# One-core attention and mixture-of-experts kernel: the first expert tile's products placed between the last two attention pairs' products

## The chip, the cores and the metric

The kernel runs on one core of a Trainium2 chip. The core has five engines that follow their own instruction streams and meet through semaphores: TensorE (PE, with its weight loads shown apart as PEld), VectorE (DVE), ScalarE (ACT), GpSimd (POOL) and SyncE (SP). The metric is the time of one execution in microseconds on the device.

## The reference

The input x holds 128 sequences of 64 rows of width 128. Everything is in float32.

```python
x = x + attention(layernorm(x), ctx, ctx, Wq, Wk, Wv, Wo, bo, mask)   # 16 heads of 64, causal
z = layernorm(x + attention...) * ln_g + ln_b        # ffn's own layernorm of the sum
probs = softmax(z @ rW + rb)                         # 8 experts
w = top-2 of probs, normalised
hid = gelu(z @ W1[e] + b1[e]);  outs = hid @ W2[e] + b2[e]
x = x + sum over the two chosen experts of w * outs
```

## The kernel before

**Attention.** The 8192 rows are worked off as 64 *pairs* of sequences (128 rows each), four pairs to a *group*, 16 groups. The program numbers pairs from 0, and `NP` is 64, so the last two pairs are NP-2 = 62 and NP-1 = 63. For each pair TensorE makes the value products (`V` units), the scores (L1045), the transposes of the probabilities of the pair before (`T` units, L997), the products of those with the values (`attend`, L1014, 64 small 64x64 products) and the output projection (`project`, L1029, 8 products of float32 that the profile lists as 16 rows). VectorE subtracts the row maxima from the scores (L1325, L1327) and counts on the semaphore `shifted`; ScalarE takes the exponential (L773); VectorE normalises (L1333 to L1337), counting on `probs`. ScalarE copies the transposes to `pT` (L754) and the result of `attend` to `oT` (L768). VectorE adds the projection to the residual (`add_attention`, L1318). Routing of the rows to experts (`route_a`, `route_b`, `route_c`) and the scatter of normed rows to `slots` (POOL L618, one indirect DMA for each 128 rows) run in the same groups.

**Experts.** The sorted rows lie in `slots` in tiles of 256 rows, 67 tiles, each of one expert. For tile s: SP loads it to `zin` (L456); TensorE transposes it (`rows_t`, L1148, 2 products) and signals `ct_ps`; ScalarE copies the high part to `z_hi` (`hi_part`, L839); VectorE makes the low part `z_lo` (`lo_part`, L1634, signals `cl_lo`) and copies the expert's weights (`weights`, L1625 to L1627, signals `wc_ok`); TensorE makes the first products (`up`, three-part split, L914, L915 and L918 with `Ah` and `Al`, 6 products, signals `up_ps`); ScalarE takes gelu (`hidden`, L846, signals `gl_ok`); TensorE makes the second products (`down`, L1166 and L1171, signals `dn_ps`); ScalarE copies them out (`results`, L854, signals `yv_ok`); POOL scatters them to `mixed` (L702, two indirect DMAs). VectorE also works out where the rows go (`destinations` and `places`, L1640 to L1651).

**Order.** Each engine's order is the order in which the code is written. At the end of attention TensorE does, for the last group's fourth pair: the routing's rank products, `fold_b1` (L1081, 16 products one column wide), V, `attend` of pair 62, then tile 0's `rows_t`, `project` of pair 62, the T units of pair 63, `attend` of pair 63, tile 0's `up`, `project` of pair 63, and then the tiles. VectorE does `weights` and `lo_part` of tile 0 after the normalisation of pair 63. PSUM has 8 banks: banks 0 to 4 are a ring for the units of attention, banks 5 and 6 (`s_ps`) hold scores, bank 7 the projection. The buffers of the tiles (`zin`, `w_f`, `hid`, `z_hi`) lie over buffers of attention that are no longer read.

## Time and profile before

| | |
|---|---|
| three runs | 1013.84, 1015.98 and 1017.59 us |
| median | 1015.98 us |
| the profiled execution's own time | 1021.77 us |
| its span from first to last instruction | 1020.0 us |
| mean granted TensorE clock | 0.959 |
| busy PE / DVE / ACT / POOL | 909.9 / 730.4 / 617.6 / 463.9 us |

The profiled execution has 1.77 us around its span, and is 5.79 us above the median of the three runs. A busy share is an average over stages. TensorE has 660.45 us busy in the first 700 us, 94%, and less in the expert tiles behind it.

### The profile page before, as it was taken

The numbers are of one execution on the slowest core, as the hardware profiler recorded it, in microseconds if no ns is written. First come the engines' busy times: TensorE is split into PE (matmuls) and PEld (weight loads), VectorE is DVE, ScalarE is ACT, GpSimd is POOL, SyncE is SP. The second block draws the span as 40 slices with busy tenths as digits, with TensorE's granted clock in tenths as the row PEclk, the third lists the DMA queues.
The fourth block names the chain that finished last, engine by engine and source line by source line (L and its number), as shares of the span: only waits on it lengthen the run. The fifth ranks groups of instructions, "written<-read, shape, count | busy, mean of one in ns | idle before, by whom it ended". The sixth has DMA issues, their size and how long they took to land.

```text
span 1020.0 us, 36053 instructions
## 1 busy us (share of the span) xinstructions
PE 909.9 (89%) x13532; PEld 794.6 (78%) x13532; DVE 730.4 (72%) x2240; ACT 617.6 (61%) x1330; POOL 463.9 (45%) x571
## 2 busy tenths in 40 slices
PE   8999999999999999999999999999887889887870
PEld 6788888888888888888888888888776778776760
DVE  5887876778777777778778778786756565445773
ACT  5785667567656766667666756766444444354662
POOL 3432644435364543436364443533445545544562
PEclk9999999999999999999999999999987889998985
DMA  8000010101010010101001010001022322224555
GB/s 257 14 23 21 26 36 8 36 5 36 8 39 28 13 34 8 36 5 36 23 24 31 10 37 6 26 8 36 17 64 74 92 82 77 68 71 136 170 186 193
DMA packets 53401, 53.59 MB, mean 53 GB/s; under 512 B 6983, under 2 KB 46705, under 8 KB 53329
## 3 DMA queue, kind: packets, MB, share of 16 engines
q1 hardware_dynamic: 44891, 35.84, 12.4%
q0 software_dynamic: 8128, 16.79, 4.9%
q8 instruction: 36, 0.59, 0.2%
q14 instruction: 36, 0.29, 0.1%
q10 hardware_dynamic: 310, 0.08, 0.0%
HBM read 30.52 MB, written 22.17 MB: 52 GB/s over the span
## 4 chain that ended last, share of the span: by engine, by line
PE 75%; issue 7%; DVE 6%; ACT 4%; another core or an unknown queue 4%; DMA 2%; DVEq 1%; POOL 0%; SPq 0%; POOLq 0%; ACTq 0%
PE bank L1029 12%; PE bank L914 10%; PE bank L918 10%; PE bank L915 9%; PE bank L1045 9%; PE bank L1014 7%; PE bank L997 5%; PE bank L1171 4%; PE bank L1201 2%; PE bank L967 1%; PE bank L1148 1%; PE bank L942 1%; ACT pr L846 1%; DMA c_in<-in_ctx_dram 1%
## 5 line engine op out<-in xcount | busy, mean ns | idle before, releaser
L914 PE MATMUL bank<-in_h,Ah 128*128 128x256 f32 x646 | 208.0, 322 | 19.6 <-DVE Al L1634 17.1
L773 ACT ACTIVATE pr<-pr 128x512 f32<-128x512 f32 x128 | 80.4, 628 | 231.0 <-DVE pr L1327 231.0
L702 POOL DMA_INDIRECT mixed<-kf,ix_i x134 | 133.1, 994 | 125.1 <-DVE ix_i L1651 90.8
L726 ACT ACTIVATE kf<-bank 128x512 f32<-128x512 f32 x256 | 156.6, 612 | 8.1 <-PE bank L918 4.1
L914 PEld LDWEIGHTS bank<-in_h,Ah 128*128 128x128 f32 x646 | 125.7, 195 | 27.3 <-DVE Al L1634 21.4
L618 POOL DMA_INDIRECT slots<-zrow,slot_ix x120 | 126.1, 1051 | 45.3 <-issue 27.9
L1325 DVE TENSOR_REDUCE mx<-bank 128x8 f32<-128x512 f32 x128 | 87.7, 685 | 81.1 <-PE bank L1045 81.0
L918 PE MATMUL bank<-in_h,Al 128*128 128x256 f32 x512 | 145.0, 283 | 0.0
L915 PE MATMUL bank<-in_l,Ah 128*128 128x256 f32 x512 | 144.6, 282 | 0.0
L1045 PEld LDWEIGHTS bank<-kf 64*64 64x64 f32 x4096 | 81.8, 134 | 66.8 <-issue 65.6
L1029 PE MATMUL bank<-wo_s,oT 128*128 128x128 f32 x1024 | 132.7, 283 | 0.6 <-ACT oT L768 0.6
L1045 PE MATMUL bank<-kf 64*64 64x64 f32 x4096 | 102.9, 224 | 31.1 <-issue 30.4
L553 POOL TENSOR_TENSOR idle_p<-half 128x1 f32<-128x1 f32 x120 | 28.9, 243 | 214.5 <-DVE slot_ix L1423 174.9
L1029 PEld LDWEIGHTS bank<-wo_s,oT 128*128 128x128 f32 x1024 | 120.6, 193 | 5.2 <-ACT oT L768 1.0
L1337 DVE TENSOR_TENSOR pr<-pr,ri 128x512 f32<-128x512 f32 x128 | 114.1, 892 | 4.4
L1171 PE MATMUL bank<-kf,pr 128*128 128x128 f32 x536 | 85.2, 307 | 18.4 <-ACT pr L846 18.4
L558 POOL TENSOR_TENSOR rs<-ve,half 128x4 f32<-128x4 f32 (+1 forms) x32 | 43.6, 1361 | 125.0 <-DVE ve L1259 89.5
L915 PEld LDWEIGHTS bank<-in_l,Ah 128*128 128x128 f32 x512 | 97.9, 191 | 0.0
L918 PEld LDWEIGHTS bank<-in_h,Al 128*128 128x128 f32 x512 | 97.2, 190 | 0.0
L1171 PEld LDWEIGHTS bank<-kf,pr 128*128 128x128 f32 x536 | 71.6, 208 | 27.4 <-ACT pr L846 19.8
L1014 PEld LDWEIGHTS bank<-pT,vf 64*64 64x64 f32 x4096 | 69.9, 136 | 28.5 <-issue 26.0
L1327 DVE TENSOR_TENSOR pr<-bank,mx 128x512 f32<-128x512 f32 x128 | 88.5, 692 | 4.4
(202 smaller groups left out, 2009.6 us busy)
## 6 DMA issues: line engine op xcount, KB each, us to landing
kf<-slots SPq DMA_DIRECT2D x67, 130.0 KB
kf<-mixed SPq DMA_DIRECT2D x11, 512.0 KB
xs<-in_x_dram SPq DMA_DIRECT2D x16, 256.0 KB
c_in<-in_ctx_dram SPq DMA_DIRECT2D x16, 256.0 KB
out_dram<-xs SPq DMA_DIRECT2D x16, 256.0 KB
mixed<-kf,ix_i POOLq DMA_INDIRECT x134
vf<-mixed SPq DMA_DIRECT2D x4, 512.0 KB
slots<-zrow,slot_ix POOLq DMA_INDIRECT x120
```

The source lines that it names most:

```text
L618: pool.indirect_dma_start(out=slots, out_offset=bass.IndirectOffsetOnAxis(ap=ix[:, k, t:t + 1], axis=0), in_=rows[:, t, :], in_offset=None ...
L702: pool.indirect_dma_start(out=mixed, out_offset=bass.IndirectOffsetOnAxis(ap=ix_i[buf][:, j:j + 1], axis=0), in_=y_sb[buf][:, j, :], in_of ...
L726: act.activation(kfs[par][:, 2 * u:2 * u + 2, :], ring[gr.bank(name)].rearrange("p (h t) -> p h t", h=2), ACT.Copy).then_inc(act_ev, 1)
L914: pe.matmul(ps, lh, rh, start=True, stop=False)
L915: pe.matmul(ps, lh, rl, start=False, stop=False)
L918: return pe.matmul(ps, ll, rh, start=False, stop=True)
L1014: last = pe.matmul(into[b][place, S * j:S * j + S], vf[par][seq, 2 * j + h2, :], pT[seq, j, 64 * (h2 ^ b):64 * (h2 ^ b) + 64], start=True, ...
L1029: last = pe.matmul(o_ps[:, 0:D], oT[:, j, :], wo_s[:, j, :], start=(j == 0), stop=(j == H // 2 - 1))
L1045: last = pe.matmul(s_ps[b][place, S * j:S * j + S], kfs[par][dims, j, toks], kfs[par][dims, H // 2 + j, toks], start=False, stop=True, ski ...
L1171: last = pe.matmul(into[:, j, :], hid[deep][:, c, j * P:(j + 1) * P], w_f[deep][:, c * D:(c + 1) * D], start=False, stop=(c == FC - 1), sk ...
L1327: dve.tensor_tensor(by_seq(par, t), src, mx[:, par, hs].unsqueeze(2).to_broadcast([P, 8, S]), ALU.subtract).then_inc(shifted, 1)
L1337: dve.tensor_tensor(by_seq(par, t), by_seq(par, t), ri[:, par, hs].unsqueeze(2).to_broadcast([P, 8, S]), ALU.mult).then_inc(probs, 1)
```

## The change

The change reorders the end of attention and makes these helpers available earlier in the code. TensorE: `rows_t` of tile 0 moves to before `fold_b1`, and the wait for the last pair's `shifted` with it; `up` of tile 0 stands before `project` of pair 62; `rows_t` of tile 1 and `down` of tile 0 stand before `attend` of pair 63, and `up` of tile 1 right behind it. ScalarE and VectorE follow: tile 0's `hi_part` stands inside the last group, gelu of tile 0 before the copies of pair 63's T units, and the tile 0 weights and low part before the last normalisation. Tile 1's transposes and first products share bank 3; tile 0's second products go to bank 5.

```diff
+        def turned_at(s, deep):
+            return ({0: s_ps[0], 1: bank[3]}.get(s, bank[deep % 2]) if isinstance(s, int) else bank[deep % 2])[:, 0:TILE]
+        def results_at(s, deep):
+            into = s_ps[0] if isinstance(s, int) and s == 0 else bank[4 + deep % 2]
@@ ScalarE
                     exp_half(n, par, 1)
+                    if i == 3 and last:
+                        hi_part(0, 0)
...
-            hi_part(0, 0)
+            hidden(0, 0)
             for t in range(2):
                 t_unit(tail, f"T0{t}", NP - 1, t)
+            hi_part(1, 1)
+            results(0, 0)
             for b in range(2):
                 heads_unit(tail, f"O0{b}")
-            hidden(0, 0)
-            for s in range(1, NT):
+            for s in range(2, NT):
@@ TensorE
                     if i == 3 and last:
+                        pe.wait_ge(shifted, 2 * NP)
+                        rows_t(0, 0, s_ps[0])
                         fold_b1(gr)
...
-            pe.wait_ge(shifted, 2 * NP)
-            rows_t(0, 0, s_ps[0])
+            up(0, 0, s_ps[1])
             project(NP - 2, group_of(NG - 1, last=True).done("O31", 0))
             for t in range(2):
                 t_half(tail, f"T0{t}", NP - 1, 1, t)
+            rows_t(1, 1, bank[3])
+            down(0, 0)
             heads_free(tail, 0)
             attend(tail, 0, 1)
-            up(0, 0, s_ps[1])
+            up(1, 1, bank[3])
             project(NP - 1, tail.done("O01", 0))
-            rows_t(1, 1, bank[1])
-            down(0, 0)
-            for s in range(2, NT):
+            rows_t(2, 2, bank[0])
+            for s in range(3, NT):
                 tile_products(s)
@@ VectorE
                     if i == 3 and last:
+                        e = expert_of(0)
+                        first_weights(e)
+                        lo_part(0, 0)
                         dve.wait_ge(unit, gr.done("RB"))
...
+                        dve.wait_ge(dve_ev, gr.done("RB", 1))
+                        weights(0, 0, e)
                     normalize_half(n, par, 0)
...
-            weights(0, 0, expert_of(0))
-            lo_part(0, 0)
+            destinations(0, 0)
+            places(0, 0)
             add_attention(NP - 2)
             weights(1, 1, expert_of(1))
-            destinations(0, 0)
-            places(0, 0)
+            lo_part(1, 1)
             add_attention(NP - 1)
             for s in range(ADD_FROM):
                 tile_in(s, s)
```

The next listing is TensorE's order before, from pair 63's scores to tile 1's first products (`in_h,Ah` and `Al,Ah` are the first products of a tile, `kf,pr` the second, `ident,kf` a tile's transposes; `x8` of `wo_s,oT` is one `project`).

```order
L1081 MATMUL bank<-vec_cols,w_raw 128x1 x16
L914 MATMUL bank<-Vh,in_h 128x512
L915 MATMUL bank<-Vl,in_h 128x512
L918 MATMUL bank<-Vh,in_l 128x512
L1014 MATMUL bank<-pT,vf 64x64 x32
L1148 MATMUL bank<-ident,kf 128x128 x2
L1029 MATMUL bank<-wo_s,oT 128x128 x8
L997 MATMUL bank<-ident,pr 128x128 x8
L1014 MATMUL bank<-pT,vf 64x64 x32
L914 MATMUL bank<-in_h,Ah 128x256
```

The same stretch of TensorE in the changed kernel.

```order
L1096 MATMUL bank<-ident,kf 128x128 x2
L1087 MATMUL bank<-vec_cols,w_raw 128x1 x16
L920 MATMUL bank<-Vh,in_h 128x512
L921 MATMUL bank<-Vl,in_h 128x512
L924 MATMUL bank<-Vh,in_l 128x512
L1020 MATMUL bank<-pT,vf 64x64 x32
L920 MATMUL bank<-in_h,Ah 128x256
```

Behind those first products of tile 0 (six rows in all, of which the first stands above) the changed kernel goes on so.

```order
L1035 MATMUL bank<-wo_s,oT 128x128 x8
L1003 MATMUL bank<-ident,pr 128x128 x8
L1096 MATMUL bank<-ident,kf 128x128 x2
L1176 MATMUL bank<-w_b,ones_b 128x256
L1181 MATMUL bank<-kf,pr 128x128 x4
L1020 MATMUL bank<-pT,vf 64x64 x32
L920 MATMUL bank<-in_h,Ah 128x256
```

No product is added or removed: two sets of transposes, two sets of first products and one of second products change places. On VectorE, between the last group's `slot_ix` and the normalisation (`sm`, `ri`, `pr`), the changed kernel has this.

```order
L1432 CAST slot_ix<-rq 128x8
L1526 TENSOR_LOAD tile_e_i
L1526 ISA x2
L1550 ISA
L1550 COPY Ah<-w_parts 128x512
L1542 TENSOR_TENSOR Al<-bank,in_h 128x256
L1595 TENSOR_TENSOR experts<-bank,vec_cols 128x8x2
L1534 ISA
L1534 COPY kf<-experts 128x258
L1535 ISA
L1535 COPY w_b<-b_parts 3x128
L1342 TENSOR_REDUCE sm<-pr 128x8
```

Before, only the addition to `experts` stood between `slot_ix` and that normalisation; the others came behind it.

## Rows read from the trace of the kernel before

**Rows 1.** The page: the chain that ended last, share of the span by engine

```profile
PE 75%; issue 7%; DVE 6%; ACT 4%; another core or an unknown queue 4%; DMA 2%; DVEq 1%; POOL 0%; SPq 0%; POOLq 0%; ACTq 0%
```

**Rows 2.** Two stretches: length, busy (x instructions) of PE, PEld, DVE, ACT, POOL; PEclk, DMA

```profile
734.00:746.00 12.00, 6.96 (x97) 5.88 (x94) 3.21 (x12) 3.35 (x8) 6.73 (x7) 0.78 0.16 51
746.00:752.00 6.00, 6.00 (x42) 5.63 (x40) 2.18 (x11) 3.60 (x8) 0.00 (x0) 0.79 0.03 5
```

**Rows 3.** TensorE in order of time: start us, us, line, [idle before <-releaser]

```profile
727.35 3.71 PE L1081 MATMUL bank<-vec_cols,w_raw 128*128 128x1 f32 x32
...
732.07 1.99 PE L1014 MATMUL bank<-pT,vf 64*64 64x64 f32 x64
733.99 0.69 PE L1148 MATMUL bank<-ident,kf 128*128 128x128 f32 x2
735.25 2.05 PE L1029 MATMUL bank<-wo_s,oT 128*128 128x128 f32 x16 [0.57 <-ACT oT L768]
...
739.27 1.01 PE L1014 MATMUL bank<-pT,vf 64*64 64x64 f32 x34 [1.09 <-ACT pT L754]
741.48 0.28 PE L1014 MATMUL bank<-pT,vf 64*64 64x64 f32 x2 [1.20 <-issue]
742.92 0.45 PE L1014 MATMUL bank<-pT,vf 64*64 64x64 f32 x3 [1.17 <-issue]
744.33 0.97 PE L1014 MATMUL bank<-pT,vf 64*64 64x64 f32 x25 [0.96 <-issue]
745.23 0.58 PE L914 MATMUL bank<-in_h,Ah 128*128 128x256 f32 x1
...
746.68 2.80 PE L1029 MATMUL bank<-wo_s,oT 128*128 128x128 f32 x16
...
749.63 0.28 PE L1166 MATMUL bank<-w_b,ones_b 3*128 3x256 bf16 x1
...
750.83 0.38 PE L1148 MATMUL bank<-ident,kf 128*128 128x128 f32 x2
...
752.52 0.39 PE L914 MATMUL bank<-in_h,Ah 128*128 128x256 f32 x1 [0.37 <-DVE Al L1634]
```

**Rows 4.** The chain in order of time, an earlier pair's attend

```profile
720.48 1.09 PE bank L1014 x64
```

**Rows 5.** VectorE in order of time

```profile
727.45 0.69 DVE L1327 TENSOR_TENSOR pr<-bank,mx 128x512 f32<-128x512 f32 x1
...
733.69 0.69 DVE L1337 TENSOR_TENSOR pr<-pr,ri 128x512 f32<-128x512 f32 x1
...
749.51 0.29 DVE L1318 TENSOR_TENSOR xs<-bank,xs 128x128 f32<-128x128 f32 x1 [10.03 <-PE bank L1029]
...
750.25 0.42 DVE L1634 TENSOR_TENSOR Al<-bank,in_h 128x256 fp32r<-128x256 f32 x1
...
752.06 0.40 DVE L1634 TENSOR_TENSOR Al<-bank,in_h 128x256 fp32r<-128x256 f32 x1
```

**Rows 6.** ScalarE in order of time, around tile 0's gelu

```profile
745.32 1.09 ACT L768 ACTIVATE oT<-bank 128x512 f32<-128x512 f32 x2 [6.10 <-PE bank L1014]
746.42 1.28 ACT L846 ACT_TABLE_LOAD   x1
747.72 0.84 ACT L846 ACTIVATE pr<-bank,kf 128x256 f32<-128x256 f32 x2
```

**Rows 7.** POOL in order of time, its last scatter to slots and first to mixed

```profile
741.91 0.96 POOL L618 DMA_INDIRECT slots<-zrow,slot_ix  x1 [0.30 <-issue]
752.19 0.96 POOL L702 DMA_INDIRECT mixed<-kf,ix_i  x1 [9.31 <-DVE ix_i L1651]
```

**Rows 8.** SP's loads of tiles 0 to 3

```profile
705.20 3.65 SPq L456 DMA_DIRECT2D kf<-slots  x4
```

**Rows 9.** Who waited for whom, PE, 0 to 700 us: total us, times, longest

```profile
PE bank L1045 <- issue: 29.3, 73, 0.5
```

**Rows 10.** Who waited for whom, all engines, 724 to 1020 us

```profile
ACT pr L846 <- remote: 27.9, 8, 5.1
```

More of the change, by code:

```diff
@@ L779, in seed, with hi_part @@
                                scale=NEG).then_inc(seeded, 1)
+            def hi_part(s, deep):
+                act.wait_ge(ct_ps, s + 1)
+                if not isinstance(s, int) or s >= DEEP:
+                    act.wait_ge(up_ps, s - DEEP + 1)
+                act.activation(z_hi[deep], turned_at(s, deep), ACT.Copy).then_inc(ch_hi, 1)
             def group(g, first=False, last=False):
@@ L1083, in fold_b1, with rows_t @@
                 last.then_inc(unit, 1)
+            def rows_t(s, deep, into):
+                pe.wait_ge(zi[deep], 4 * (s - deep) + 16)
+                if not isinstance(s, int) or s >= 2:
+                    pe.wait_ge(cl_lo, s - 1)
+                for j in range(TJ):
+                    last = pe.transpose(into[:, j * P:(j + 1) * P], zin[deep][:, j, 0:D], ident[:, :])
+                last.then_inc(ct_ps, 1)
             def group(g, first=False, last=False):
@@ L1142, in _ @@
             group(NG - 1, last=True)
-            def rows_t(s, deep, into):
-                pe.wait_ge(zi[deep], 4 * (s - deep) + 16)
-                if not isinstance(s, int) or s >= 2:
-                    pe.wait_ge(cl_lo, s - 1)
-                for j in range(TJ):
-                    last = pe.transpose(into[:, j * P:(j + 1) * P], zin[deep][:, j, 0:D], ident[:, :])
-                last.then_inc(ct_ps, 1)
             def up(s, deep, into):
@@ L1162, in down @@
             def down(s, deep):
+                if isinstance(s, int) and s == 1:
+                    pe.wait_ge(yv_ok, 1)
                 if not isinstance(s, int) or s >= 2:
                     pe.wait_ge(yv_ok, s - 1)
-                into = bank[4 + deep % 2][:, 0:TJ * D].rearrange("p (j d) -> p j d", d=D)
+                into = results_at(s, deep)
                 pe.matmul(into, ones_b[0:3, :], w_b[deep][:, :].unsqueeze(1).to_broadcast([3, TJ, D]),
@@ L1514, in _, with expert_of, weights, lo_part @@
             SURE, REST = slice(0, FULL), slice(FULL, NT)
+            def expert_of(s):
+                return dve.value_load(tile_e_i[0:1, bass.ds(s, 1)], min_val=0, max_val=E - 1)
+            def weights(s, deep, e):
+                src = experts[:, bass.ds(e, 1), :].rearrange("p a c -> p (a c)")
+                if not isinstance(s, int) or s >= DEEP:
+                    dve.wait_ge(dn_ps, s - DEEP + 1)
+                if not isinstance(s, int) or s:
+                    dve.tensor_copy(w_r[deep], w1_parts[:, bass.ds(e, 1), :].rearrange("p a c -> p (a c)")).then_inc(wc_ok, 1)
+                dve.tensor_copy(w_f[deep], src[:, 0:B2]).then_inc(wc_ok, 1)
+                dve.tensor_copy(w_b[deep][:, :], b2_parts[:, bass.ds(e, 1), :].rearrange("p a d -> p (a d)")).then_inc(
+                    wc_ok, 1)
+            def lo_part(s, deep):
+                dve.wait_ge(ch_hi, s + 1)
+                if not isinstance(s, int) or s >= DEEP:
+                    dve.wait_ge(up_ps, s - DEEP + 1)
+                dve.tensor_tensor(z_lo[deep], turned_at(s, deep), z_hi[deep].bitcast(F32),
+                                  ALU.subtract).then_inc(cl_lo, 1)
+            def first_weights(e):
+                dve.wait_ge(e2_ok, E)
+                dve.wait_ge(b2_ok, 6)
+                dve.wait_ge(ld_e, 16 * E)
+                dve.tensor_copy(w_r[0], w1_parts[:, bass.ds(e, 1), :].rearrange("p a c -> p (a c)")).then_inc(wc_ok, 1)
             def group(g, first=False, last=False, tables=None):
@@ L1611, in _ @@
             dve.wait_ge(w1_ok, 2)
-            dve.wait_ge(dve_ev, group_of(NG - 1, last=True).done("RB", 1))
-            dve.wait_ge(e2_ok, E)
-            dve.wait_ge(b2_ok, 6)
-            dve.wait_ge(ld_e, 16 * E)
-            def expert_of(s):
-                return dve.value_load(tile_e_i[0:1, bass.ds(s, 1)], min_val=0, max_val=E - 1)
-            def weights(s, deep, e):
-                src = experts[:, bass.ds(e, 1), :].rearrange("p a c -> p (a c)")
-                if not isinstance(s, int) or s >= DEEP:
-                    dve.wait_ge(dn_ps, s - DEEP + 1)
-                dve.tensor_copy(w_r[deep], w1_parts[:, bass.ds(e, 1), :].rearrange("p a c -> p (a c)")).then_inc(wc_ok, 1)
-                dve.tensor_copy(w_f[deep], src[:, 0:B2]).then_inc(wc_ok, 1)
-                dve.tensor_copy(w_b[deep][:, :], b2_parts[:, bass.ds(e, 1), :].rearrange("p a d -> p (a d)")).then_inc(
-                    wc_ok, 1)
-            def lo_part(s, deep):
-                dve.wait_ge(ch_hi, s + 1)
-                if not isinstance(s, int) or s >= DEEP:
-                    dve.wait_ge(up_ps, s - DEEP + 1)
-                dve.tensor_tensor(z_lo[deep], (bank[deep % 2] if s else s_ps[0])[:, 0:TILE], z_hi[deep].bitcast(F32),
-                                  ALU.subtract).then_inc(cl_lo, 1)
             def destinations(s, deep):
@@ L1653, in tile_in @@
             def tile_in(s, k):
-                if s:
+                if not isinstance(s, int) or s > 1:
                     lo_part(s, k % DEEP)
```

17 lines of the change are left out of this document (4 added, 13 removed).

## The prediction

> **What bounds the kernel now.** I read the page's chain first: 75% of it is TensorE, 7% is "issue", time in which TensorE mostly has nothing that the profile shows to wait for [rows 1]. So only what shortens TensorE's path near the change can count. Then the stretches: from 734 to 746 us TensorE is busy 6.96 of 12 us, idle for 5.04, and from 746 to 752 it is busy throughout, both at a mean granted clock near 0.78, a mix of the two levels 2.4 and 1.2 GHz [rows 2]. The change can fill those 5 us and perhaps keep the clock up; it cannot take out work, since the order listing has the same products before and after.
>
> In order of time the idle pieces are these [rows 3]: 0.57 us before the projection of pair 62, which waits for ScalarE's `oT`; 1.09 us before pair 63's `attend`, which waits for `pT`; and then 1.20, 1.17 and 0.96 us *inside* that `attend`, with "issue" as releaser. It starts at 739.27 and ends at 744.33 + 0.97 = 745.30, so 6.03 us for 64 products that took 1.09 us for an earlier pair [rows 4]. This stall of 4.94 us is the largest thing in the place of the change, and no semaphore explains it.
>
> What stands beside it is on POOL: scatters to `slots` run one after another until 741.91 + 0.96 = 742.87 [rows 7], and the `attend` runs freely again only from 744.33. Small products show the same kind of gap in the groups: the 64x64 score products lose 29.3 us in 73 gaps of at most 0.5 us to "issue" [rows 9]. Larger products beside scatters show none: the projection at 735.25 took 2.05 us. I take it that a burst of 64x64 products suffers when POOL issues indirect DMAs, and that larger ones do not.
>
> **The change part by part.** I follow TensorE from 727.35, where `fold_b1` began, to the first products of tile 2, which began at 752.52 [rows 3]. At that point both kernels have done the same products (transposes of tiles 0 to 3, first products of 0 and 1, second products of 0), and go on in the same order. The difference of that one time is the change's direct effect.
>
> 1. *Transposes of tile 0 ahead of `fold_b1`, with the wait for `shifted`.* VectorE ends the last shift at 727.45 + 0.69 = 728.14 [rows 5], and the transposes cost up to 0.69 [rows 3]; the tile has been loaded since 708.85 [rows 8]. `fold_b1` starts near 728.8 in place of 727.35: 1.4 us later. Before, the wait cost nothing, as `fold_b1` hid it. Queued behind it are V and `attend` of pair 62, which end at 735.5 in place of 734.06. The transposes' old place gives nothing back: it lay in the wait for `oT`.
>
> 2. *VectorE.* Weights' high part, `lo_part`, and two weight copies now stand before the last normalisation, which ended at 734.38 [rows 5]. It starts after `fold_b1` as before (1.4 us later) and the two copies add about half a microsecond (the `w_f` and `w_b` copies between two `lo_part`s; all of the work between the two `lo_part`s of 750.25 and 752.06 is under 1.81 us), so it ends by 736.4. Its consumer, the T units, comes after 738. Cost nothing; only beyond 2 us more would it be on the path.
>
> 3. *First products of tile 0 before the projection of pair 62.* They stand in the wait for `oT`, which lasted 735.25 - 734.06 = 1.19 us, 0.57 of it idle and the rest the tile's transposes. Six of them took 746.68 - 745.23 = 1.45 us at the low clock, about 0.85 at the high clock (752.52's like, estimated from 0.39 for the first). So they cost nothing or 0.26. Projection 62 starts at 736.65, and the T units end 2.9 us later (739.27 - 1.09 - 735.25), at 739.6.
>
> 4. *Transposes of tile 1 and second products of tile 0 before `attend` 63.* 0.38 and 750.83 - 749.63 = 1.20 us: ready at 741.1, in place of 739.27. The old wait for `pT`, 1.09, lies under them. They need gelu of tile 0. ScalarE starts its table load after `oT`'s copies and the exponential, about 736.9; 1.28 and 0.84 [rows 6] give 739.0, in time for 739.9. So `attend` 63 starts 1.85 us later.
>
> Here a rule of the Trainium skill may be weighed. In the rows the gelu starts at 747.72, straight after the load of 1.28 us, and the load straight after the copy that ends at 746.41 [rows 6]. The Trainium skill (ScalarE: Activation LUTs, What ACT_TABLE_LOAD costs) says that a switch costs 1.38 us of drain on top, 2.66 us in all. By the row `attend` 63 starts at 741.1; by the page the gelu ends near 740.4 and `pT`'s two copies queue behind it, so that it starts at 741.9, and the gain is 0.8 less. The trace doesn't show that drain, so I go by the row.
>
> 5. *`attend` 63 to tile 2's first products.* Before: 752.52 - 745.30 = 7.22 us, of it tile 0's first products 1.45, the projection 2.80 and 3.04 from the projection's end at 749.48. After: first products of tile 1 lie under `oT`'s copies (1.09 [rows 6], 1.2 with its semaphore), projection 2.05 at the high clock or 2.80 at the low. Then comes a wait that takes the place of a filled stretch: the transposes of tiles 2 and 3 take 0.7 us, but tile 2's `lo_part` is queued on VectorE behind `add_attention` of pair 63, the places of tiles 1 and 2 and tile 2's weights. Before, `lo_part` of tile 2 began at 752.06, 2.55 us after that addition began at 749.51 [rows 5]; only tile 1's `lo_part` (0.42, less overlap) has left the row. So tile 2's first products start 2.7 us after the projection's end, with some 2 us of TensorE idle. Sum 1.2 + 2.05 + 2.7 = 5.95 us at the high clock, and 1.45 + 2.8 + 2.7 = 6.95 at the low.
>
> With d for the length of `attend` 63 the join stands at 741.1 + d + 5.95 = 747.05 + d, so **the gain is 5.47 - d** at the high clock, 4.47 - d at the low. The bounds of d: 1.09 [rows 4] without a stall, gain 4.4; 6.03 if the stall goes along whole, loss 0.6, or 1.6 with the low clock; more, if POOL's work grows under it (rival 2). Between them I take that the stall ends with POOL's scatters as it did before, so that the burst is over at about 745.3 wherever it began: d = 4.2, gain 1.3. Part of it at the low clock leaves about **1 us**.
>
> Against my reading of d, the Trainium skill (SBUF — State Buffer, Who interferes with whom) says that DMA never contends with a compute engine. By it the gaps would belong to the run of products itself, d stays 6.03, and the change loses 0.6 us. No row tells which instruction or descriptor holds the issue, only that the times coincide.
>
> *The profile against the runs.* The sum is made against a span of 1020.0 in an execution of 1021.77 us. The three runs have a median of 1015.98, 5.79 less, which is about the size of the stall of 4.94. If runs without the profiler don't have it, the join was at 747.6 before and is at 748.1 now, 0.6 us later: no change again. My forecast is 1016 less 1: 1015 us. What remains behind the join (65 tiles) depends on it only through one another, so I carry the difference at full size.
>
> **The rivals.**
> - *Forecast, 0.45:* the stall's end stays put or it fades, gain 0 to 4.5 us, 1011.5 to 1016.
> - *Rival 1, the full gaps filled, and the clock too, 0.12:* d = 1.1, and the clock is full through the projection: gain 4.4, and up to 1 us more if the tiles behind start at the high clock. 1010.5 to 1011.6. For it: TensorE is nearly without idle from 728 to 741. Against it: scatters run to 742.87 whatever the change does.
> - *Rival 2, the stall goes along and grows, 0.30:* tile 0's results now exist at 741.5, so POOL goes on from `slots` to `mixed` without a pause, where it had begun at 752.19 [rows 7]. Two more scatters of 1.27 us each push their end to 745.4; with the lag of 2.43 that the burst's end had behind the last scatter it ends at 747.8, d = 6.7, loss 1.2, and 2.2 at the low clock. It decides once POOL starts on `mixed` before the burst is over. 1016 to 1018.5.
> - *Rival 3, the other side, slower by over 0.5%, 0.08:* the tile phase has eight waits of ScalarE's gelu for something the profile doesn't name, 27.9 us, the longest 5.1 [rows 10]. Scatters and loads now begin earlier against it; one or two more such waits on the chain cost 5 to 9 us: 1021 to 1025. The same waits falling off the chain could give as much the other way (0.05).
> - *No effect at all* is rival 2 and the forecast meeting at zero: by the filled pieces alone, 0.57 and 1.09 us, the change gives less than its new waits (1.4 and 2) take.
>
> **How the numbers follow.** About 0.5%, 5.1 us, is what a measurement of this kernel can tell from no change: below 1010.9 is faster, above 1021.1 slower. The direct effect is bounded by +4.4 (5.4 with the clock) and -2.2, so it reaches the lower bound only at its very end: about half of rival 1 and the lucky share of rival 3, 0.11. Slower 0.09. The likeliest case's own range is 1011.5 to 1016. Range for all: from 1010 (rival 1 whole) to 1019.5 (rival 2, and 1.5 for the scatter of the runs).
>
> **What would show it.** `fold_b1` starts 1.3 to 1.5 us after the rank products; first products of tile 0 directly behind `attend` 62, no idle before projection 62; the table load before the T copies, and no wait before `attend` 63; the number of gaps in `attend` 63, with POOL's scatters beside them: this decides. Behind the last projection an idle piece of about 2 us released by `lo_part` (L1634's twin). I am wrong if the last normalisation becomes the release of the T units, if the gelu comes late for tile 0's second products, or if POOL's scatters move. The direct effect would be right and the total wrong if the join moves as said, but the time from it to the end (1020.0 - 752.52 = 267.5 us) changes by more than 3 us.

## The result and the profile after

| | before | changed |
|---|---|---|
| median of 17 runs each | 1015.98 us | 1021.18 us |
| lowest and highest | 1009.48, 1018.76 | 1015.75, 1027.89 |
| the profiled execution's own time | 1021.77 | 1020.31 |
| its span | 1020.0 | 1018.6 |

The ratio is 1.0053, with a 95% interval of 1.0032 to 1.0073: 5.2 us slower, where 1 us faster was forecast. The two profiled executions stand the other way round, because they differ by 4.2 us before the change begins: the rank products ahead of `fold_b1`, up to which both programs are the same, start at 727.14 in the one and at 722.97 in the other. So I measure from there.

The chain of the changed kernel's page is of the same kind as before [rows 1]:

```profile
PE 76%; issue 7%; DVE 6%; ACT 4%; another core or an unknown queue 4%; DMA 1%; POOL 1%; DVEq 0%; POOLq 0%; ACTq 0%; SPq 0%
```

TensorE after, in order of time; L1087 is `fold_b1`, L1020 `attend`, L1035 `project`, L1003 the T units, L1096 a tile's transposes, L920 to L924 its first products, L1176 and L1181 its second:

```profile
722.97 0.18 PE L985 MATMUL bank<-chosen_b,upper_b 128*128 128x32 bf16 x1
...
724.01 0.44 PE L1096 MATMUL bank<-ident,kf 128*128 128x128 f32 x2 [0.70 <-DVE pr L1336]
724.29 5.67 PE L1087 MATMUL bank<-vec_cols,w_raw 128*128 128x1 f32 x32
...
731.38 2.10 PE L1020 MATMUL bank<-pT,vf 64*64 64x64 f32 x51
733.72 0.48 PE L1020 MATMUL bank<-pT,vf 64*64 64x64 f32 x4 [0.24 <-issue]
...
737.35 0.50 PE L1020 MATMUL bank<-pT,vf 64*64 64x64 f32 x4 [0.95 <-issue]
738.78 0.57 PE L920 MATMUL bank<-in_h,Ah 128*128 128x256 f32 x1 [0.94 <-issue]
...
741.57 3.78 PE L1035 MATMUL bank<-wo_s,oT 128*128 128x128 f32 x16 [0.57 <-ACT oT L775]
...
748.06 1.16 PE L1020 MATMUL bank<-pT,vf 64*64 64x64 f32 x64
...
750.41 2.05 PE L1035 MATMUL bank<-wo_s,oT 128*128 128x128 f32 x16 [0.28 <-ACT oT L775]
752.30 0.60 PE L1096 MATMUL bank<-ident,kf 128*128 128x128 f32 x4
755.50 0.39 PE L920 MATMUL bank<-in_h,Ah 128*128 128x256 f32 x1 [2.60 <-DVE Al L1542]
```

Against [rows 3]: `attend` of pair 63 is clean, 1.16 us in place of 6.03. But `attend` of pair 62 now has the gaps. It takes from 731.38 to 737.85, 6.47 us, where it had taken 1.99. Tile 0's first products start after another gap, and the projection takes 3.78 us in place of 2.05. POOL's scatters to `slots` (L625), second and last, and ScalarE's `oT` copies (L775) of the same kernel:

```profile
730.26 0.97 POOL L625 DMA_INDIRECT slots<-zrow,slot_ix  x1 [3.27 <-issue]
...
737.86 0.96 POOL L625 DMA_INDIRECT slots<-zrow,slot_ix  x1 [0.30 <-issue]
```

```profile
740.43 1.09 ACT L775 ACTIVATE oT<-bank 128x512 f32<-128x512 f32 x2 [8.35 <-remote]
```

The scatters have not moved: the second starts 7.3 us behind the rank products here and 7.2 before. `attend` 62 has: it began 4.93 us behind them and was over when the second scatter started, and now begins 8.41 behind them, inside the row of scatters. Of these 3.48 us, 1.11 are the wait and the transposes ahead of `fold_b1`; the rest is `fold_b1` (5.67 us in place of 3.71) and V, which ran at the low clock. ScalarE's copy also comes late, 2.6 us after `attend` 62's end, where it had followed at once.

The stretches, with the granted clock as the number behind the five busy times [rows 2]:

```profile
724.00:746.00 22.00, 17.92 (x128) 15.55 (x129) 6.13 (x23) 5.80 (x11) 7.75 (x8) 0.54 0.10 31
746.00:756.00 10.00, 7.12 (x110) 6.20 (x110) 3.94 (x19) 4.23 (x10) 1.92 (x2) 1.00 0.10 29
```

From 724 to 746 us the mean granted clock is 0.54: nearly all of it at the 1.2 GHz level. The clock fell at about 725.5, inside `fold_b1`, and rose at 746.0, so the low stretch is 20.5 us long; in the kernel before there were two, 10 us in all. TensorE had been idle 0.70 us and had then run the transposes and 1.2 us of the thin products before it fell; the gaps beside the scatters came while it was low.

The **join**, tile 2's first products, is 755.50 - 722.97 = 32.53 us behind the rank products, and was 752.52 - 727.14 = 25.38: 7.15 us later. Behind the join the changed kernel's execution takes 263.1 us and the other 267.5. That part differs much between executions: in the 18 profiled executions of this document it runs from 258.6 to 270.3 us.

Piece by piece the 7.15 us are these. The second profile of the changed kernel (`a_beside`, experiment 8) was read in the same way.

| TensorE, us later than before | changed | `a_beside` |
|---|---|---|
| rank products to the start of `fold_b1` | +1.11 | +1.10 |
| `fold_b1` | +1.96 | +0.60 |
| its end to `attend` 62 (V) | +0.41 | +0.41 |
| `attend` 62 and `attend` 63 together | -0.39 | -0.63 |
| end of `attend` 62 to projection 62 (wait for `oT`) | +2.53 | +4.02 |
| start of projection 62 to `attend` 63 | +2.47 | +3.22 |
| end of `attend` 63 to the join | -0.94 | -0.95 |
| join | +7.15 | +7.77 |

So the gaps moved from one `attend` to the other and cost about the same there: `attend` 62 is 4.48 us longer, `attend` 63 4.87 us shorter. What makes the join late is what lies around them: the wait, ScalarE's late copy, and products at the low clock. `fold_b1`, projection 62 and the T units behind it took 4.12 us more in all (5.67, 3.78 and 1.47 in place of 3.71, 2.05 and 1.04).

### The profile page after: what moved, and what is told of

The parts are those of the page before. It is cut to its first block, busy times and chain, and to the rows that moved or that the text cites. A ratio compares the mean times of both kernels' runs of the same rounds, so it can differ in the third digit from the quotient of the medians.

```text
span 1018.6 us, 36053 instructions
## 1 busy us (share of the span) xinstructions
PE 910.5 (89%) x13532; PEld 793.4 (78%) x13532; DVE 731.3 (72%) x2240; ACT 618.8 (61%) x1330; POOL 465.0 (46%) x571
## 4 chain that ended last, share of the span: by engine, by line
PE 76%; issue 7%; DVE 6%; ACT 4%; another core or an unknown queue 4%; DMA 1%; POOL 1%; DVEq 0%; POOLq 0%; ACTq 0%; SPq 0%
PE bank L1035 12%; PE bank L920 10%; PE bank L924 10%; PE bank L921 9%; PE bank L1051 9%; PE bank L1020 7%; PE bank L1003 5%; PE bank L1181 5%; PE bank L1211 2%; PE bank L973 1%; PE bank L948 1%; PE bank L1096 1%; ACT pr L855 1%; DVE xs L1706 1%
## 5 line engine op out<-in xcount | busy, mean ns | idle before, releaser
L920 PE MATMUL bank<-in_h,Ah 128*128 128x256 f32 x646 | 206.9, 320 | 19.8 <-DVE Al L1542 16.4
L920 PEld LDWEIGHTS bank<-in_h,Ah 128*128 128x128 f32 x646 | 124.6, 193 | 28.2 <-DVE Al L1542 19.6
L625 POOL DMA_INDIRECT slots<-zrow,slot_ix x120 | 125.8, 1049 | 44.9 <-issue 28.9
L924 PE MATMUL bank<-in_h,Al 128*128 128x256 f32 x512 | 144.5, 282 | 0.0
L1035 PE MATMUL bank<-wo_s,oT 128*128 128x128 f32 x1024 | 133.0, 284 | 0.9 <-ACT oT L775 0.9
L1035 PEld LDWEIGHTS bank<-wo_s,oT 128*128 128x128 f32 x1024 | 120.7, 194 | 5.5 <-ACT oT L775 1.4
L924 PEld LDWEIGHTS bank<-in_h,Al 128*128 128x128 f32 x512 | 96.9, 189 | 0.0
L1181 PE MATMUL bank<-kf,pr 128*128 128x128 f32 x536 | 82.9, 301 | 11.7 <-ACT pr L855 9.7
L1020 PEld LDWEIGHTS bank<-pT,vf 64*64 64x64 f32 x4096 | 70.2, 136 | 26.7 <-issue 25.4
L1342 DVE TENSOR_REDUCE sm<-pr 128x8 f32<-128x512 f32 x128 | 86.7, 677 | 0.0
```

The lines of the kernel that those rows point to most:

```text
L625: pool.indirect_dma_start(out=slots, out_offset=bass.IndirectOffsetOnAxis(ap=ix[:, k, t:t + 1], axis=0), in_=rows[:, t, :], in_offset=None ...
L920: pe.matmul(ps, lh, rh, start=True, stop=False)
L924: return pe.matmul(ps, ll, rh, start=False, stop=True)
L1020: last = pe.matmul(into[b][place, S * j:S * j + S], vf[par][seq, 2 * j + h2, :], pT[seq, j, 64 * (h2 ^ b):64 * (h2 ^ b) + 64], start=True, ...
L1035: last = pe.matmul(o_ps[:, 0:D], oT[:, j, :], wo_s[:, j, :], start=(j == 0), stop=(j == H // 2 - 1))
L1181: last = pe.matmul(into[:, j, :], hid[deep][:, c, j * P:(j + 1) * P], w_f[deep][:, c * D:(c + 1) * D], start=False, stop=(c == FC - 1), sk ...
```

## The experiments

Each kernel was timed beside the kernel before on the same chip, 10 to 12 runs of its own. Three chips were used, called A (experiments 1 to 3), B (4 to 7) and C (8). The kernel before had a median of 1015.84 us on A, 1022.63 and 1023.65 on B and 1021.95 on C, so only ratios to before are compared. They are good to about 0.3%; where two kernels are compared through their ratios, the difference is good to some 0.4%, 4 us. I call the two parts of the change that turned out to matter the *early transposes* (tile 0's `rows_t`, with its wait, ahead of `fold_b1`) and the *late low part* (tile 2's `lo_part` queued on VectorE behind pair 63's addition).

**1. Early transposes alone, in the kernel before** (`b_rows_first`).

```diff
                     if i == 3 and last:
+                        pe.wait_ge(shifted, 2 * NP)
+                        rows_t(0, 0, s_ps[0])
                         fold_b1(gr)
...
-            pe.wait_ge(shifted, 2 * NP)
-            rows_t(0, 0, s_ps[0])
             project(NP - 2, ...)
```

> The kernel before with one part of the change alone: tile 0's transposes, with the wait for the last shift, stand on TensorE ahead of fold_b1. Theory A (clock): the wait of some 0.7 us, the two transposes and the 16 one-column products together let the clock fall before fold_b1 ends; fold_b1 takes 5 to 5.7 us in place of 3.71, the projection and the products behind it run at the low clock for 10 us or more, and the kernel is 3 to 7 us slower than before. Theory B (scatter collision): the clock does not matter; attend of pair 62 is pushed by 1.4 us only, most of it stays ahead of the scatters, and the kernel is 1 to 3 us slower. If neither holds and the loss sits in the later part of the change, this kernel is within 1.5 us of before.

Measured 1.0043 (1.0014 to 1.0072), 4.4 us: this step can carry most of the loss, and the size is that of theory A. `fold_b1` took 4.72 us. In the profile `attend` 62 is clean (1.99 us) although it ran beside the second scatter, but ScalarE's `oT` copies begin late, and TensorE waits for them:

```profile
738.57 3.65 PE L1029 MATMUL bank<-wo_s,oT 128*128 128x128 f32 x16 [4.47 <-ACT oT L768]
```

`attend` 63 comes behind the scatters and is clean too, so the join is only 1.2 us later than before. One execution doesn't show the mean of twelve.

**2. Early transposes taken back, in the changed kernel** (`a_rows_behind`).

```diff
-                        pe.wait_ge(shifted, 2 * NP)
-                        rows_t(0, 0, s_ps[0])
                         fold_b1(gr)
+                        pe.wait_ge(shifted, 2 * NP)
+                        rows_t(0, 0, s_ps[0])
@@ ScalarE
-                    if i == 3 and last:
-                        hi_part(0, 0)
...
+                    if i == 3 and last:
+                        hi_part(0, 0)
```

> The changed kernel with that one part taken back to behind fold_b1 (ScalarE's high part then behind the T copies); all else as changed. Theory A: fold_b1 takes 3.7 us again, the clock falls later and for a shorter time, attend of pair 62 ends before most scatters: 3 to 6 us faster than the changed kernel, about level with before. Theory B: attend 62 starts earlier by 1 us or so and meets fewer scatters: 1 to 3 us faster than the changed kernel. If the loss is the new wait for tile 2's low part behind the last projection (2.60 us idle), this kernel keeps the whole loss of 5 us.

Measured 1.0003 (0.9977 to 1.0029): the loss is gone, 5 us by the ratios, again the size of theory A. `fold_b1` took 4.12 us and ends 4.32 us behind the rank products, `attend` 62 is clean, `attend` 63 takes 2.37 us, and the join is at 24.7. The wait for tile 2's low part is still there, so that wait alone does not make the 5 us.

**3. Scatters held, in both kernels** (`a_hold`, `b_hold`). On POOL, in each:

```diff
-            send_rows(zrow, slot_ix, 0, 2 * GP)
+            send_rows(zrow, slot_ix, 0, 1)
+            pool.wait_ge(unit, end.done("O31"))     # attend 62 done
+            send_rows(zrow, slot_ix, 1, 4)
+            pool.wait_ge(unit, tail.done("O01"))    # attend 63 done
+            send_rows(zrow, slot_ix, 4, 2 * GP)
```

> The changed kernel with POOL's scatters held: the second to fourth wait for the end of attend 62, the last four for the end of attend 63. No scatter overlaps a burst of 64x64 products. Scatter theory: attend 62 takes 2.0 us (low clock) or 1.1 in place of 6.5, no issue gaps in either attend or in tile 0's first products, 3 to 5 us faster than the changed kernel. Rival (the gaps belong to straight-line code or to the profile's own records): the same number of gaps as before and no change in time.

> The kernel before with POOL's scatters held the same way; only attend 63 is touched by it. Scatter theory: attend 63 takes 1.1 to 2 us in place of 6.03 and the kernel is 3 to 5 us faster than before, faster than any other here. Rival (gaps belong to the run of products or to the profile): attend 63 still has its gaps, or the gaps go and the runs do not get faster, within 1.5 us of before.

Measured 0.9962 (0.9936 to 0.9988) and 0.9931 (0.9907 to 0.9955): 9 us faster than the changed kernel by the ratios, and 7 us faster than before. `attend` 63 in the kernel before with scatters held, and POOL's row there:

```profile
735.27 3.78 PE L1033 MATMUL bank<-wo_s,oT 128*128 128x128 f32 x16 [0.57 <-ACT oT L772]
...
740.88 1.16 PE L1018 MATMUL bank<-pT,vf 64*64 64x64 f32 x64 [0.74 <-ACT pT L758]
```

```profile
738.52 0.96 POOL L618 DMA_INDIRECT slots<-zrow,slot_ix  x1 [0.30 <-issue]
742.38 0.96 POOL L618 DMA_INDIRECT slots<-zrow,slot_ix  x1 [2.89 <-PE bank L1018]
```

The same 64 products, in the same code, take 1.16 us when no scatter lies beside them and 6.03 when they do. That settles that the scatters make the gaps inside `attend`, and the ratios say that they cost time in runs without the profiler too. So the prediction's guess that runs without the profiler might not have them was wrong.

The two ratios say one thing more. With the scatters held in both, the changed kernel is still 0.31% behind the kernel before, 3 us, give or take some 3.5. So how much of its 5 us the scatters make can't be read from this pair.

**4. Thin products widened** (`a_wide_fold`), a test of the clock.

```diff
-                    last = pe.matmul(ring[gr.bank("RB")][:, u:u + 1], w1_raw[...], bc, ...)
+                    last = pe.matmul(ring[gr.bank("RB")][:, 32 * u:32 * u + 32], w1_raw[...],
+                                     bc_wide[:, 0:32], ...)
```

> The changed kernel with the 16 products of fold_b1 made 32 columns wide instead of one, same weights, same place (VectorE reads every 32nd column). Clock theory: the granted clock stays at its high level through fold_b1, or its low stretch is clearly shorter than the 20.5 us of the changed kernel; fold_b1 takes about 4 us in place of 5.67, projection 62 takes 2.05 in place of 3.78, and the kernel is 2 to 4 us faster than the changed kernel. Collision theory alone: the low stretch may change but attend 62 still falls under the scatters, and the time changes by less than 1.5 us.

Measured 1.0048 (1.0018 to 1.0077), no better than the changed kernel. `fold_b1` took 5.10 us, and the low clock came in two stretches of 6.8 and 10.2 us in place of one of 20.5. So the low clock lasted 17.0 us in place of 20.5 and the time did not change. That is a weak test: the clock moved too little to judge it by. Where the time went stands behind tile 0's first products:

```profile
738.03 0.28 PE L924 MATMUL bank<-in_h,Ah 128*128 128x256 f32 x1
743.40 3.78 PE L1035 MATMUL bank<-wo_s,oT 128*128 128x128 f32 x16 [5.09 <-ACT oT L775]
```

TensorE ran tile 0's first products at the high clock and then waited 5.09 us for ScalarE. `attend` 62 had its gaps here too (4.67 us), and ScalarE's copy began at 742.27, 4.9 us after it and 1.2 us after the last scatter to `slots`.

**5. Both at once** (`a_behind_hold`, transposes behind `fold_b1` and scatters held; `b_rows_hold`, before with early transposes and scatters held). Their edits are those of 1, 2 and 3.

> The changed kernel with tile 0's transposes behind fold_b1 and POOL's scatters held around both attends. If the cost of the early transposes is mostly the collision, removing both brings little over holding alone: about 1012, as the changed kernel with scatters held (1012.5). If it is mostly wait and clock, the two add: 1009 to 1010.5, about level with before with scatters held (1010.3).

> The kernel before with tile 0's transposes ahead of fold_b1 and the scatters held. Its distance to before with scatters held (1010.3) is the cost of that step without a collision: 1.1 us for the wait and the transposes that show in the trace, plus what the clock adds. Collision theory: 1 to 1.5 us, 1011.5. Clock theory: 3 to 4.5 us, 1013.5 to 1015.

Measured 0.9939 (0.9906 to 0.9971) and 0.9981 (0.9952 to 1.0011). Times 1015.84, the median that the expectations count from, these are 1009.6 and 1013.9 us. Both lie where the expectation puts wait and clock, 1009 to 1010.5 and 1013.5 to 1015, and not where it puts the collision, 1012 and 1011.5. The intervals (1006.3 to 1012.9, and 1011.0 to 1017.0) hold both theories, and the join of `b_rows_hold`, 22.8 us, is no later than that of `b_hold`, 23.2. So it isn't shown that the early transposes cost nothing once the scatters are held; if anything these two point to a cost of their own. `a_hold_in` below, 0.9943 beside the 0.9949 of the same kernel with the transposes behind, points the other way.

**6. The late low part taken back** (`a_behind_hold_in` on top of 5, `a_in` in the changed kernel alone). On VectorE:

```diff
             lo_part(1, 1)
+            tile_in(0, 0)
+            tile_in(1, 1)
             add_attention(NP - 1)
             for s in range(ADD_FROM):
-                tile_in(s, s)
+                if s >= 2:
+                    tile_in(s, s)
```

> As the changed kernel with transposes behind fold_b1 and scatters held, and on VectorE the places of tiles 1 and 2 and tile 2's weights moved ahead of the addition of pair 63's attention, which they had queued behind. The wait of 2.60 us on TensorE for tile 2's low part falls to below 0.8 and the kernel is 1.5 to 2.5 us faster than without this; if what is filled here is given back behind, the wait goes and the time stays within 1 us.

> The changed kernel with only the VectorE order altered: places of tiles 1 and 2 and tile 2's weights ahead of the addition of pair 63's attention. If the 2.60 us wait for tile 2's low part carries through to the end, 2 to 2.6 us faster than the changed kernel, ratio 1.0025 to 1.0035. If time filled at the start of the tiles is given back behind, ratio 1.0045 to 1.006 as the changed kernel, with the join of tile 2's first products 2 us or more earlier in the trace.

Measured 0.9949 (0.9928 to 0.9971) and 0.9996 (0.9964 to 1.0029). On top of 5 it brought nothing that could be measured (0.9939 without it), though the trace shows the wait gone; here is the place in `a_behind_hold_in`:

```profile
745.59 0.60 PE L1100 MATMUL bank<-ident,kf 128*128 128x128 f32 x4
746.90 0.39 PE L924 MATMUL bank<-in_h,Ah 128*128 128x256 f32 x1 [0.71 <-issue]
```

The join came 2.7 us earlier (19.6 in place of 22.3 us) and the ratio did not follow. That the time filled there was given back in the tiles is not shown: the two intervals leave room for the 2.7 us. In the changed kernel alone the same edit brought 4 to 6 us, more than the 2.60 us of the wait. In its profile `attend` 62 began 7.04 us behind the rank products, not 8.41, and was clean, although the second scatter was issued 0.29 us after it began; ScalarE was late instead:

```profile
744.74 1.08 ACT L761 ACTIVATE pT<-bank 128x512 f32<-128x512 f32 x2 [4.02 <-remote]
...
750.13 1.08 ACT L775 ACTIVATE oT<-bank 128x512 f32<-128x512 f32 x2 [3.75 <-remote]
```

The edit stands behind `attend` 62 in the order of every engine, so it is hardly what kept that clean.

**7. Which wait, which hold** (`a_hold62`, `b_wait`, `b_hold_late`).

```diff
# a_hold62, POOL, changed kernel
+            send_rows(zrow, slot_ix, 0, 1)
+            pool.wait_ge(unit, end.done("O31"))
+            send_rows(zrow, slot_ix, 1, 2 * GP)
# b_wait, TensorE, kernel before
+                        pe.wait_ge(shifted, 2 * NP)
                         fold_b1(gr)
# b_hold_late, POOL, kernel before
+            send_rows(zrow, slot_ix, 0, 1)
+            pool.wait_ge(unit, tail.done("O01"))
+            send_rows(zrow, slot_ix, 1, 2 * GP)
```

> The changed kernel, where POOL's second to eighth scatter wait for the end of attend 62 and nothing else; the early transposes stay. If the loss of the changed kernel is that attend 62 (and the first products and ScalarE's oT copy behind it) came under the scatters, this alone takes it back to level with before, ratio 0.998 to 1.002, with attend 62 at 2.0 us and the gaps now in attend 63 or behind. If the loss is the wait for the shift, the transposes and the clock, attend 62 is clean and the ratio stays at 1.003 to 1.005.

> The kernel before with only the wait for the last shift ahead of fold_b1; the transposes stay where they were. With the transposes moved too, the ratio was 1.0043 and the trace showed 1.1 us more ahead of fold_b1. If the wait itself is the cost (it delays fold_b1 by some 0.8 us, opens a gap ahead of the thin products and moves attend 62 toward the scatters), ratio 1.002 to 1.005. If the cost is the transposes' new place or no real effect of this step, ratio 0.999 to 1.0015.

> The kernel before with the second to eighth scatter held to behind attend 63, so that none of them lies beside either attend, projection 62, the T units or ScalarE's copies. Scatter theory: at least as good as holding in two parts (0.9931): 0.990 to 0.995, unless seven scatters in one row beside the first tiles delay the first scatters to mixed, which then would give back 1 to 3 us: 0.994 to 0.998. Rival (the gain of holding was noise of the runs): within 0.998 to 1.002.

`a_hold62` measured 1.0022 (0.9991 to 1.0053), inconclusive between its two theories, but its profile is the clearest of all. `attend` 62 is clean, and `attend` 63 meets scatters to `slots` and then, without a pause, to `mixed`:

```profile
741.20 0.69 PE L1022 MATMUL bank<-pT,vf 64*64 64x64 f32 x30
742.93 0.37 PE L1022 MATMUL bank<-pT,vf 64*64 64x64 f32 x5 [1.05 <-issue]
...
748.68 0.49 PE L1022 MATMUL bank<-pT,vf 64*64 64x64 f32 x4 [0.94 <-issue]
```

```profile
745.02 0.96 POOL L625 DMA_INDIRECT slots<-zrow,slot_ix  x1 [0.30 <-issue]
746.28 0.96 POOL L711 DMA_INDIRECT mixed<-kf,ix_i  x1 [0.30 <-issue]
747.54 0.96 POOL L711 DMA_INDIRECT mixed<-kf,ix_i  x1 [0.30 <-issue]
```

It takes 9.59 us: the gaps last about as long as POOL issues, to 748.50, and the last of them ends 1.6 us later. This is rival 2 of the prediction, gaps that go along and grow, in a kernel that has it.

`b_wait` measured 1.0014 (0.9982 to 1.0046): not told from zero, nor from 2 to 4 us. Its join is 3.5 us late, with TensorE idle for 4.95 us before projection 62.

`b_hold_late` measured 0.9994 (0.9968 to 1.0020), against 0.990 to 0.998 by the scatter theory; it falls in the range of the rival, that the gain of holding was noise, which experiment 8 then speaks against. The join is 1.6 us earlier than before and both attends are clean, but behind the join ScalarE's gelu of tile 1 comes late, and TensorE waits for it:

```profile
756.95 0.95 POOL L704 DMA_INDIRECT mixed<-kf,ix_i  x1 [0.30 <-issue]
```

```profile
759.02 0.84 ACT L848 ACTIVATE pr<-bank,kf 128x256 f32<-128x256 f32 x2 [6.79 <-remote]
```

```profile
759.91 2.08 PE L1173 MATMUL bank<-kf,pr 128*128 128x128 f32 x8 [5.98 <-ACT pr L848]
```

The first line is the last of nine scatters that POOL issued without a pause from 746.83 to 757.90, seven to `slots` and two to `mixed`; `b_hold` has a pause in the same row and no such wait of ScalarE's there. So in this execution the stall was not taken away but moved onto ScalarE. That *where* the scatters are put decides what holding them is worth is shown by the two ratios, 0.9994 and 0.9931.

**8. On one chip** (`a_beside`, the changed kernel itself; `a_behind_in`, both parts taken back; `a_hold_in`, scatters held and low part early; `b_hold_beside`, as `b_hold`).

> The changed kernel itself, as the anchor for the three beside it on this chip. If its loss does not depend on the chip, ratio 1.003 to 1.007 again. If it does, the earlier comparison of parts across chips says nothing of sizes. Its profile is also a second look at where the scatters' stall falls: in attend 62, in ScalarE's copies behind it, or in attend 63.

> The changed kernel with the transposes behind fold_b1 and the VectorE order altered, scatters free. If the two costs add, 5 us from the one and 2 to 5 from the other, ratio 0.994 to 0.998. If they are the same microseconds counted twice (what one gives the other can't), ratio 0.999 to 1.001.

> The changed kernel, early transposes kept, scatters held around both attends, VectorE order altered. Join theory (the time is set by when tile 2's first products start): join at about 20.5 us behind the rank products, 5 us before that of the kernel before, ratio 0.993 to 0.996. If the early transposes cost something beyond the join, ratio 0.997 to 1.000, above the 0.9949 of the same kernel with the transposes behind.

> The kernel before with the scatters held in two parts, once more, now beside the changed kernel. Scatter theory: ratio 0.992 to 0.995 again and 9 to 12 us ahead of the changed kernel. If the first result was luck of that chip or of those runs, 0.998 to 1.001, as the kernel with all seven scatters held to behind attend 63 (0.9994).

Measured 1.0040 (1.0011 to 1.0069), 0.9996 (0.9968 to 1.0024), 0.9943 (0.9917 to 0.9969) and 0.9955 (0.9930 to 0.9981). The changed kernel's second profile repeats the first: `attend` 62 takes 6.23 us, ScalarE's copy is 4.1 us late, the join is at 33.15. The two parts taken back together give what each gave alone, so they are not two sums to add. `b_hold_beside` is 9.8 us ahead of the changed kernel on this chip, so the gain of holding is no noise. With the scatters held, the changed order with the low part early (0.9943) and the order before (0.9955) come out level, ahead of both kernels; without that VectorE edit the changed order had 0.9962 against 0.9931 (experiment 3).

All of it in one table, sorted by the join; `attend` lengths and join are those of one profiled execution, the ratio that of the runs. All lengths are in us.

| kernel | attend 62 | attend 63 | join behind ranks | ratio | chip |
|---|---|---|---|---|---|
| `a_beside` | 6.23 | 1.16 | 33.2 | 1.0040 | C |
| `a_wide_fold` | 4.67 | 1.16 | 32.8 | 1.0048 | B |
| changed | 6.47 | 1.16 | 32.5 | 1.0053 | not told |
| `a_hold62` | 1.99 | 9.59 | 31.9 | 1.0022 | B |
| `a_in` | 1.99 | 1.99 | 29.3 | 0.9996 | B |
| `b_wait` | 2.43 | 1.16 | 28.8 | 1.0014 | B |
| `a_behind_in` | 1.99 | 1.16 | 27.6 | 0.9996 | C |
| `b_rows_first` | 1.99 | 1.16 | 26.6 | 1.0043 | A |
| before | 1.99 | 6.03 | 25.4 | 1 | |
| `a_rows_behind` | 1.99 | 2.37 | 24.7 | 1.0003 | A |
| `b_hold_late` | 1.99 | 1.16 | 23.8 | 0.9994 | B |
| `a_hold` | 1.99 | 1.34 | 23.3 | 0.9962 | A |
| `b_hold_beside` | 1.99 | 1.16 | 23.2 | 0.9955 | C |
| `b_hold` | 1.99 | 1.16 | 23.2 | 0.9931 | A |
| `b_rows_hold` | 1.89 | 1.16 | 22.8 | 0.9981 | B |
| `a_behind_hold` | 1.99 | 1.43 | 22.3 | 0.9939 | B |
| `a_hold_in` | 1.99 | 1.47 | 21.2 | 0.9943 | C |
| `a_behind_hold_in` | 1.99 | 1.16 | 19.6 | 0.9949 | B |

The join orders the ratios only in coarse steps. Beyond 32 us they are 1.004 to 1.005; from 32 to 23.8 us all but one lie between 0.9994 and 1.0022, whatever the join; and the held kernels from 23.3 us down have 0.993 to 0.998, with nothing more gained below. One execution's join stands here against some twelve runs, and where the stall falls differs: `b_rows_first` doesn't fit for this reason or for another.

## Why the prediction was wrong

**The step that failed is step 1**, "Queued behind it are V and `attend` of pair 62, which end at 735.5 in place of 734.06". The delay ahead of `fold_b1` was priced about rightly: 1.1 us by 724.29 - 722.97 against the 0.21 of before, forecast 1.4. But I let everything behind it keep its length: `fold_b1` and V, which took 2.4 us more at the low clock, and `attend` 62 with its 1.99 us. Before, it ended at 734.06, 0.25 us ahead of the second scatter; I had POOL's row of scatters in hand, used it for `attend` 63, and did not ask what the delayed burst would run into. It ran into the same scatters and took 6.47 us. In the terms of the sum, `attend` 62 ended 14.88 us behind the rank products, where I had 8.4 (735.5 - 727.14): 7.96 us later than before and not 1.4.

**Step 3 failed with it**, "they cost nothing or 0.26", by which projection 62 follows `attend` 62 after some 1.2 us. It followed after 3.72 us in the first profile and 5.21 in the second, since ScalarE's copy began 2.6 and 4.1 us late. Then the projection took 3.78 us in place of 2.05, at the low clock. `fold_b1` took 5.67 and 4.31 us in place of 3.71, for the low clock began in it, before any gap of the scatters. The forecast had nothing for either. What the clock costs by itself stays open: widening the thin products did not help the time, but hardly shortened the low stretch, and experiments 1, 2 and 5 came out at the sizes expected for the clock.

**Step 5, with the formula 5.47 - d**, was about right in its parts and useless as a total. d came out near its lower bound, 1.16 against 1.09, by luck: everything before `attend` 63 was so late that it began 9.2 us after the last scatter to `slots` had ended. I had counted on scatters until 742.87 beside it. From `attend` 63's end to the join it took 755.50 - 749.22 = 6.28 us, forecast 5.95; the new wait for tile 2's low part is 2.60, forecast some 2. By the formula the gain would have been 4.3. The start was 25.1 behind the rank products and not 14.0.

**Steps 2 and 4, and the rest of 3.** The last normalisation was no release of anything. Tile 0's first products stood in the wait for `oT` as said, but the wait was 3.7 us. And there was idle time before projection 62, 0.57 us, which the prediction said would be gone. The gelu's table load took 1.28 us with the gelu straight behind it (741.65, 742.95), in line with the row and not with the longer figure of the Trainium skill (ScalarE: Activation LUTs, What ACT_TABLE_LOAD costs).

**The reading of the gaps.** That POOL's indirect DMAs make them is now shown (experiment 3), against the rule of the Trainium skill that I weighed (SBUF — State Buffer, Who interferes with whom): by that rule DMA never contends with a compute engine, and the 4.9 us that vanish with the scatters moved show that something of an indirect DMA does, whether or not it is SBUF's ports. What I added, "larger ones do not", is only half true. Before tile 0's first products there was a gap of 0.94 us. Nor is it true of every small burst: in `a_rows_behind`, `a_in` and `b_rows_first` `attend` 62 ran beside one scatter or two and kept its 1.99 us. ScalarE's late copies lie in the same stretches, and in four kernels they end 1.1 to 1.6 us after POOL's last scatter, as the gaps in `attend` 63 do before (1.5 us) and in `a_hold62` (1.6 us); that they have the same cause is likely, but waits of this kind stand all through the expert tiles and no run separates them. The runs have the stall too, without the profiler.

**The rivals.** Rival 2 had the right mechanism, scatters under a burst on the path, and the wrong burst and price: it capped the loss at 2.2 us. The measured 1021.18 us lies in the band of rival 3, 1021 to 1025 us at 0.08, by luck: ScalarE's unnamed waits in the tiles did not grow. From 757 us on they come to 53.0 us in the changed kernel and 54.7 in the one before. The one that mattered stood ahead of the tiles, before `oT`. The bounds that I gave the direct effect, a gain of 4.4 and a loss of 2.2 us, were none, since it held all bursts but one at their old lengths.

**The total.** The join moved by 7.15 us and the runs by 5.2. I had carried the join's difference at full size; with 258.6 to 270.3 us behind the join from one execution to another, no single profile can test that. What stays open: how the 5.2 us divide between the scatters, the low clock and ScalarE's copy, and why taking back either the early transposes or the late low part undoes the loss alone. The second has no way to act on `attend` 62, yet its runs were level with before. Perhaps a shorter chain behind hides part of the stall, but no run here settles it. Nor is it settled what in the issue of an indirect DMA holds the other engines' queues.

## What to carry to other kernels

When a step is delayed, price what it will run into and not only how much later it ends: here 1.1 us of delay, and 2.4 more from the low clock, moved a burst of small products under a row of scatters, which made it 4.5 us longer. If a trace shows gaps by "issue" in such a burst, look for indirect DMAs at the same time on POOL before reordering anything; putting those elsewhere was worth some 5 to 9 us in every order tried, more than any order of TensorE's work, while putting them all in one late row was worth nothing that could be measured, as the stall then fell on ScalarE. And when a stall disappears from one place in a trace, look for it on the other engines before counting it as gained.

## What the runs showed of the hardware

- Beside a row of indirect DMAs of POOL, each 0.96 us at a distance of 1.27, a burst of 64 products of 64x64 took 4.7 to 9.6 us (changed kernel, `a_beside`, `a_wide_fold`, `a_hold62`, before), in place of 1.16 at the high clock and 1.99 with the low one. The gaps are 0.2 to 1.2 us each, between runs of 1 to 5 products, and last about as long as POOL goes on issuing.
- With the scatters beside that burst held back and nothing else changed, it took 1.16 us in place of 6.03 (`b_hold`), and the kernel was 0.7 and 0.45% faster (0.9931 and 0.9955).
- In the same stretches ScalarE's instructions start late, for something that the profile doesn't name: 2.6 us (changed), 4.1 (`a_beside`), 4.9 (`a_wide_fold`), and in `b_hold_late` the gelu with an idle time of 6.79. In these four they start 1.1 to 1.6 us after the last scatter of the row has ended.
- Where the stall falls is not decided by when the burst begins against the scatters. `attend` 62 began 0.11 us ahead of the second scatter in `a_beside` and took 6.23 us. It began 0.29 us ahead of it in `a_in` and 0.16 us behind it in `b_rows_first` and was clean in both, and ScalarE was late instead. In these two the second scatter took 1.43 and 1.35 us, not 0.96.
